# Half-precision pairs for the q, k and v projections of a cross-attention and expert-layer kernel

## What is computed

```python
xn = layernorm(x)                        # over the last axis, 512
q = einsum('oc,bct->bot', Wq, xn) + bq   # 256 x 256 weights, per batch row 256 x 512
k = einsum('oc,bcs->bos', Wk, ctx) + bk
v = einsum('oc,bcs->bos', Wv, ctx) + bv
# 16 heads of 16 channels, 512 x 512 scores per head
dot = mask * (q.T k) / 4 - (1 - mask) * 1e6
x = x + (softmax(dot) * mask) @ v
```

## Time and profile before

| | |
|---|---|
| time of 3 runs, median (range) | 726.11 us (725.21 to 729.36) |
| profiled execution: time | 723.49 us |
| profiled execution: span | 721.7 us |
| mean granted TensorE clock | 0.944 of full speed |
| busy share of the span: TensorE, VectorE, ScalarE, GpSimd | 87%, 72%, 62%, 44% |
| chain that ended last, by engine | TensorE 62%, VectorE 14%, ScalarE 8%, issue 8%, DMA 4%, GpSimd 3% |

### The profile page before, as it was taken

How to read it: one execution, slowest core, us unless ns; L and a number is a source line. 1 busy time by engine, 2 the same in 40 slices (tenths; PEclk the granted TensorE clock), 3 DMA queues, 4 the chain that set the end, 5 groups by cost and what they waited for, 6 DMA issues and landing times.

```text
span 721.7 us, 11922 instructions
## 1 busy us (share of the span) xinstructions
PE 626.2 (87%) x3864; PEld 257.7 (36%) x3864; DVE 516.8 (72%) x959; ACT 448.9 (62%) x608; POOL 320.9 (44%) x444
## 2 busy tenths in 40 slices
PE   4788999999999999999999987778899799999950
PEld 3623333323333323323323221124444466664420
DVE  2497788888888898888888898742748354444674
ACT  3654878877877877878887875663522377773000
POOL 5583335355355454444533504321824644431554
PEclk9857999999999999999999996799999999999995
DMA  8533254354354355354234320042995133332454
GB/s 302 174 111 99 70 161 128 105 150 129 103 151 133 111 140 147 98 139 134 96 88 132 113 72 30 31 109 84 197 224 106 51 111 114 121 111 74 153 166 140
DMA packets 65611, 88.61 MB, mean 123 GB/s; under 512 B 12576, under 2 KB 46112, under 8 KB 64528
## 3 DMA queue, kind: packets, MB, share of 16 engines
q1 hardware_dynamic: 60992, 69.64, 31.8%
q0 software_dynamic: 4560, 18.22, 10.9%
HBM read 63.75 MB, written 32.74 MB: 134 GB/s over the span
## 4 chain that ended last, share of the span: by engine, by line
PE 62%; DVE 14%; ACT 8%; issue 8%; DMA 4%; POOL 3%; SPq 0%; POOLq 0%; ACTq 0%; DVEq 0%
PE PS L859 16%; PE PS L831 10%; PE PS L640 8%; PE PS L766 8%; PE PS L1470 6%; ACT E L845 5%; DVE MX L772 5%; PE PS L719 4%; PE PS L1067 4%; PE PS L1531 3%; DVE ST L393 2%; POOL E L1583 2%; PE PS L1440 1%; DMA E<-scr_ys,SL 1%; ACT BIG L508 1%
## 5 line engine op out<-in xcount | busy, mean ns | idle before, releaser
L772 DVE TENSOR_REDUCE MX<-PS 128x1 f32<-128x512 f32 x512 | 327.0, 684 | 53.6 <-PE PS L766 53.0
L845 ACT ACTIVATE E<-PS 128x1024 f32<-128x1024 f32 x256 | 259.3, 1020 | 80.6 <-PE PS L831 79.7
L859 PE MATMUL PS<-E,BIG 128*32 128x512 f32 x1024 | 140.6, 622 | 3.3 <-ACT E L845 3.2
L766 PE MATMUL PS<-BIG 53*128 53x512 f16 x512 | 123.1, 400 | 17.5 <-DVE MX L772 17.2
L831 PE MATMUL PS<-BIG 55*128 55x512 f16 x512 | 103.0, 397 | 23.9 <-ACT E L845 20.7
L674 POOL TENSOR_TENSOR ML<-BIG,ML 128x512 f32<-128x512 f32 x30 | 38.2, 1275 | 142.5 <-ACT BIG L650 142.5
L831 PEld LDWEIGHTS PS<-BIG 55*128 55x128 f16 x512 | 24.6, 93 | 169.6 <-ACT E L845 99.7
L650 ACT ACTIVATE BIG<-PS,BIG 128x256 f32<-128x256 f32 x64 | 36.0, 564 | 34.4 <-PE PS L640 27.8
L1424 POOL DMA_INDIRECT CT<-scr_yr,IX x39 | 37.0, 949 | 43.3 <-PE PS L1440 36.3
L1492 DVE SCALAR_TENSOR_TENSOR E<-WP,PS 128x352 bf16<-128x352 f32 x39 | 20.3, 521 | 48.8 <-ACT WP L1482 46.1
L1470 PE MATMUL PS<-BIG,CT 128*128 x312 | 53.0, 313 | 2.3 <-ACT CT L1449 1.7
(11 more groups left out here) (207 smaller groups left out, 851.1 us busy)
## 6 DMA issues: line engine op xcount, KB each, us to landing
scr_parts<-WP SPq DMA_DIRECT2D x96, 128.0 KB
BIG<-scr_parts SPq DMA_DIRECT2D x64, 192.0 KB
BIG<-in_we POOLq DMA_DIRECT2D x8, 1088.0 KB, 13.9
scr_u<-ML SPq DMA_DIRECT2D x32, 256.0 KB, 2.2
scr_ys<-XN SPq DMA_DIRECT2D x19, 256.0 KB
X<-in_x SPq DMA_DIRECT2D x8, 512.0 KB, 6.0
CT<-in_ctx SPq DMA_DIRECT2D x8, 512.0 KB, 6.1
ML<-scr_u SPq DMA_DIRECT2D x16, 256.0 KB
```

What stands on the lines that cost most here:

```text
L766: e.matmul(PS[:, yi[name] % 3, :], QK[rows, qb(u), 0, j0 + jj, 128 * tt:128 * tt + 128], QK[rows, qb(u), 1, j0 + jj, :], start=True, stop= ...
L772: e.tensor_reduce(MX[:, g % 2, c:c + 1], PS[:, yi[name] % 3, :], AX.X, ALU.max)\
L845: e.activation(E[:, st, 2 * jj:2 * jj + 2, :], PS[:, slot(name):slot(name) + 2, :], ACT.Exp, scale=1 / 1024).then_inc(s["rc"], 1)
L859: ins = e.matmul(PS[32 * hh:32 * hh + 32, AVB, :], VT[:, b % 2, st, 4 * (g % 4) + hh, :], E[:, st, hh, :], start=(st == 0), stop=(st == 3))
```

## The change

In the profile's words, from unit 4 on (batch row 2 on), so in 12 of 16 units:

- `project_whole` takes the place of `project_qk`: q and k are computed for all 512 columns in one piece, as three float16 products per half of K (high by high, high by low, low by high), 6 matmuls of 128 x 512 instead of 4 float32 matmuls of 128 x 256. It takes one place in `ring` instead of two, due at 4.25 IT (q) and 7.25 IT (k), and is made before `attend`, so that at these due times it stands just ahead of an "a". ScalarE evacuates it in one piece of 512 columns.
- v takes 6 float16 matmuls of 256 columns per part instead of 2 float32 ones; its evacuation multiplies by a scale as well as adding the bias.
- `split_weights`, once: the sums of squares of the three weights (ScalarE, TensorE, VectorE, GpSimd), the high parts (ScalarE, three, due at 0.45 units) and the low parts (VectorE, three, due at 0.7 units).
- `split_source(b)`, for batch rows 2 to 7: five small GpSimd steps and three of 1024 columns (scale in place, high part, low part), due at 6.1 IT of the unit 2b - 4.
- `split_target(b)`: two GpSimd steps of 1024 columns, due at 0.3 IT of the unit 2b - 3. The normalised rows use one buffer from batch row 2 on, since the other one holds the pair.
- `balance` gets one small VectorE step and three small GpSimd steps for the new scales.
- The context of batch row 4 and later is loaded once the split of two rows earlier is done; two later users of the memory that holds the pairs wait for the last projections.

The diff, cut to its core:

```diff
+W0 = 4
...
+        ZW, WC, WI = few[:, 40:43], few[:, 43:46], few[:, 46:49]
+        CC, IC, VS, MS, RS = (few[:, i:i + 2] for i in (49, 51, 53, 55, 57))
+        WQs = big[:, 20672:23744].bitcast(HF).rearrange("p (r a b c) -> p r a b c", r=2, a=3, b=2)
+        CTs = [v.bitcast(HF).rearrange("p (r k t) -> p r k t", r=2, k=2)
+               for v in (big[:, 17792:19840], big[:, 15360:17408])]
+        XNs = XN[:, 1, :, :].rearrange("p k t -> p (k t)").bitcast(HF).rearrange("p (r k t) -> p r k t", r=2, k=2)
...
         for w in range(NU):
-            ring += [(w - 3 + 3.75 * IT, ("q", w, 0)), (w - 3 + 4.75 * IT, ("q", w, 1)),
-                     (w - 3 + 6.75 * IT, ("k", w, 0)), (w - 3 + 7.75 * IT, ("k", w, 1))]
+            if w < W0:
+                ring += [(w - 3 + 3.75 * IT, ("q", w, 0)), (w - 3 + 4.75 * IT, ("q", w, 1)),
+                         (w - 3 + 6.75 * IT, ("k", w, 0)), (w - 3 + 7.75 * IT, ("k", w, 1))]
+            else:
+                ring += [(w - 3 + 4.25 * IT, ("q", w, 1)), (w - 3 + 7.25 * IT, ("k", w, 1))]
             tv = -1 - .25 * IT if w == 1 else w - 2 + .75 * IT
             mring += [(tv, ("v", w, 0)), (tv + (.1 if w == 1 else 2) * IT, ("v", w, 1))]
         mring.append((-3 + 3.6 * IT, ("w",)))
         mring.append((-1.26, ("z",)))
+        mring.append((.12, ("y",)))
...
                 if n < 8:
-                    if n >= 2:
-                        e.wait_ge(s["rp"], zi["q", 2 * n - 3, 1] + 1)
-                    dst = XN[:, n % 2, :, :]
+                    if n == 2:
+                        e.wait_ge(s["rp"], zi["q", 1, 1] + 1)
+                    elif n > 2:
+                        e.wait_ge(s["xq"], n - 2)
+                    dst = XN[:, 1 if n == 1 else 0, :, :]
...
+                if b >= 4:
+                    e.wait_ge(s["cs"], b - 3)
+                if b >= 2:
+                    e.tensor_scalar(MS[:, b % 2:b % 2 + 1], PS[:, bank, 0:1], 1 / 131072, 1e-30, ALU.mult, ALU.max)
...
-                e.tensor_tensor(bq, bqkc[:, 0:2], r8, ALU.mult)
+                if b >= 2:
+                    pch.step(e, e.tensor_tensor(bq, bqkc[:, 0:2], r8, ALU.mult))
+                    e.tensor_tensor(r8, r8, WI[:, 0:1].broadcast_to([128, 2]), ALU.mult)
+                else:
+                    e.tensor_tensor(bq, bqkc[:, 0:2], r8, ALU.mult)
                 pch.step(e, e.tensor_scalar(sk, sk, 256.0, None, ALU.mult))
-                e.tensor_tensor(bk, bqkc[:, 2:4], sk, ALU.mult).then_inc(s["bal"], 1)
+                if b < 2:
+                    e.tensor_tensor(bk, bqkc[:, 2:4], sk, ALU.mult).then_inc(s["bal"], 1)
+                else:
+                    pch.step(e, e.tensor_tensor(bk, bqkc[:, 2:4], sk, ALU.mult))
+                    pch.step(e, e.tensor_tensor(sk, sk, WI[:, 1:2].broadcast_to([128, 2]), ALU.mult))
+                    e.tensor_tensor(sk, sk, IC[:, b % 2:b % 2 + 1].broadcast_to([128, 2]), ALU.mult)\
+                        .then_inc(s["bal"], 1)
...
+        def split_weights():
+            name = ("y",)
+            bank = yi[name] % 3
+
+            def squares(e):
+                e.wait_ge(s["w"], 32)
+                e.wait_ge(s["w1"], 16)
+                e.wait_ge(s["w2"], 16)
+                e.wait_ge(s["mp"], yi["w",] + 1)
+                spare = big[:, 20672:21696].bitcast(F32).rearrange("p (k c) -> p k c", k=2)
+                for i, out in enumerate((SQW[:, 0, :, :], SQW[:, 1, :, :], spare)):
+                    ins = e.activation(out, WQ[:, i, :, :], ACT.Square, accum_out=ZW[:, i:i + 1])
+                ins.then_inc(s["wz"], 1)
+            act.at(-.2, squares)
+
+            def mm(e):
+                take_bank(e, name)
+                e.wait_ge(s["wz"], 1)
+                e.matmul(PS[:, bank, 0:3], OO, ZW, start=True, stop=True).then_inc(s["mp"], 1)
+            pe.at(when_at[name], mm)
+
+            def fetch(e):
+                e.wait_ge(s["mp"], yi[name] + 1)
+                e.tensor_scalar(WC, PS[:, bank, 0:3], 1 / 65536, 1e-30, ALU.mult, ALU.max).then_inc(s["mc"], 1)
+            dve.at(when_at[name] + DA, fetch)
+
+            def factor(e):
+                e.wait_ge(s["mc"], yi[name] + 1)
+                pch.step(e, e.tensor_tensor(WC, WC, mhalf[:, 0:3], ALU.pow))
+                e.tensor_scalar(WC, WC, 64.0, None, ALU.mult).then_inc(s["wf"], 1)
+            pool.at(when_at[name] + .4 * IT, factor)
+
+            def upper(e):
+                e.wait_ge(s["wf"], 1)
+                e.wait_ge(s["sw"], 1)
+                for i in range(3):
+                    e.activation(WQs[:, 0, i, :, :], WQ[:, i, :, :], ACT.Identity, scale=WC[:, i:i + 1])\
+                        .then_inc(s["wh"], 1)
+            act.at(.45, upper)
+
+            def lower(e):
+                dch.step(e, e.reciprocal(WI, WC))
+                for i in range(3):
+                    e.wait_ge(s["wh"], i + 1)
+                    e.scalar_tensor_tensor(WQs[:, 1, i, :, :], WQ[:, i, :, :], WC[:, i:i + 1], WQs[:, 0, i, :, :],
+                                           ALU.mult, ALU.subtract).then_inc(s["wq"], 1)
+            dve.at(.7, lower)
+
+        def split_source(b):
+            name = ("f", b)
+            c, ic, v = CC[:, b % 2:b % 2 + 1], IC[:, b % 2:b % 2 + 1], VS[:, b % 2:b % 2 + 1]
+            ms, r = MS[:, b % 2:b % 2 + 1], RS[:, b % 2:b % 2 + 1]
+            src = CT[:, b % 2, :, :]
+            hi, lo = (CTs[b % 2][:, i, :, :] for i in range(2))
+
+            def factors(e):
+                if b == 2:
+                    e.wait_ge(s["wq"], 3)
+                if b >= 4:
+                    e.wait_ge(s["mc"], yi["v", 2 * b - 3, 1] + 1)
+                pch.step(e, e.tensor_tensor(r, ms, mhalf[:, 0:1], ALU.pow))
+                pch.step(e, e.tensor_scalar(c, r, 64.0, None, ALU.mult))
+                pch.step(e, e.tensor_tensor(ic, ms, r, ALU.mult))
+                pch.step(e, e.tensor_scalar(ic, ic, 1 / 64, None, ALU.mult))
+                e.tensor_tensor(v, ic, WI[:, 2:3], ALU.mult).then_inc(s["cs"], 1)
+            pool.at(when_at[name] + .312 * IT, factors)
+
+            def split(e):
+                e.wait_ge(s["sqa"], b + 1)
+                if b >= 4:
+                    e.wait_ge(s["rp"], zi["k", 2 * b - 3, 1] + 1)
+                elif b == 2:
+                    e.wait_ge(s["sw"], 3)
+                pch.step(e, e.tensor_scalar(src, src, c, None, ALU.mult))
+                pch.step(e, e.tensor_copy(hi, src))
+                e.tensor_tensor(lo, src, hi, ALU.subtract).then_inc(s["cq"], 1)
+            pool.at(when_at[name] + .34 * IT, split)
+
+        def split_target(b):
+            src = XN[:, 0, :, :]
+
+            def split(e):
+                e.wait_ge(s["xn"], b + 1)
+                e.wait_ge(s["rp"], zi["q", 2 * b - 1, 1] + 1)
+                pch.step(e, e.tensor_copy(XNs[:, 0, :, :], src))
+                e.tensor_tensor(XNs[:, 1, :, :], src, XNs[:, 0, :, :], ALU.subtract).then_inc(s["xq"], 1)
+            pool.at(2 * b - 4 + 8.3 * IT, split)
+
+        def project_whole(w, i):
+            b, o = w // 2, w % 2
+            name = ("qk"[i], w, 1)
+            bank = slot(name)
+            rows = XNs if i == 0 else CTs[b % 2]
+
+            def mm(e):
+                take_slot(e, name)
+                e.wait_ge(s["cq" if i else "xq"], b - 1)
+                if w == W0:
+                    e.wait_ge(s["wq"], i + 1)
+                for kt in range(2):
+                    for a, c in ((0, 0), (0, 1), (1, 0)):
+                        ins = e.matmul(PS[:, bank, :], WQs[:, a, i, kt, 128 * o:128 * o + 128], rows[:, c, kt, :],
+                                       start=(kt == a == c == 0), stop=(kt == a == 1))
+                ins.then_inc(s["rp"], 1)
+            pe.at(when_at[name], mm)
+
+            def evac(e):
+                e.wait_ge(s["rp"], zi[name] + 1)
+                e.wait_ge(s["bal"], b + 1)
+                e.wait_ge(s["fr%d" % i], w)
+                e.activation(FB[:, i, :], PS[:, bank, :], ACT.Identity,
+                             bias=COL[:, b % 2, 4 * i + 2 + o:4 * i + 3 + o],
+                             scale=COL[:, b % 2, 4 * i + o:4 * i + o + 1]).then_inc(s["rc"], 1)
+            act.at(when_at[name] + DA, evac)
+
...
+                    n = slice(128 * st, 128 * st + 128)
                     for kt in range(2):
-                        ins = e.matmul(PS[:, bank, 0:256], CT[:, b % 2, kt, 128 * st:128 * st + 128],
-                                       WQ[:, 2, kt, :], start=(kt == 0), stop=(kt == 1))
+                        if w < W0:
+                            ins = e.matmul(PS[:, bank, 0:256], CT[:, b % 2, kt, n],
+                                           WQ[:, 2, kt, :], start=(kt == 0), stop=(kt == 1))
+                            continue
+                        for a, c in ((0, 0), (0, 1), (1, 0)):
+                            ins = e.matmul(PS[:, bank, 0:256], CTs[b % 2][:, a, kt, n], WQs[:, c, 2, kt, :],
```

(29 more changed lines are left out.)

14 lines of the change are left out of this document (9 added, 5 removed), and 2 rows, old and new, of the table s.

## The result

The changed kernel takes 763.67 us (median of four runs, 761.39 to 765.84) against 727.36 of the kernel before in the same job: a ratio of 1.052, 95% interval 1.0486 to 1.0555. It is slower, as forecast, but by 36 us where the forecast said 15.5, and it lies above the range's 757.

What follows compares the result with a forecast made beforehand. Three engines near full, chained by two slots and three banks, bound the loop, not TensorE's columns alone. Projections 10.3 + 1.4 and weights 3.8 gave 15.5 us more, 741.6 against the median; range 729 to 757.

Steps and rivals of the forecast that it cites:

- What ends a step: Main loop: the second s waits for a bank, freed by VectorE's reduction, with "a" queued behind it.
- an empty step gives back 0.42: Steps that lose a projection half: each half costs TensorE 1.06 us but the loop only 0.42.
- a whole piece at this place fills nothing: Piece at 4.25 and 7.25 IT, behind the second s: "a" and all behind it move by the full 1.39 us.
- The 24 places: Whole q and k pieces: 19 at 0.54 us more, 5 with the context's squares at 0.28 more; 10.3 + 1.4 us.
- columns count in full: Rival, main loop: bound by TensorE's issue, 25 us less and 3.8 more for the weights, 705 us; chance 0.08.
- The weights' split, once: Unit 0: high parts and context squares on ScalarE 2.3 us, low parts on VectorE 1.5; together 3.8, between 0 and 6.5.
- The low parts: Weights' split on VectorE, unit 0: three at least 0.70 us each and a small step, delaying their step by 1.5 us.
- GpSimd ... its results are needed units later, so I cost it at 0: GpSimd's splits: about 10.5 us more per batch row, from 25.3 to 36 of a period of 54, cost 0.
- Loads on SyncE are not later than before: SyncE's queue: the change makes no load later, so no cost was counted.
- The first victim: GpSimd's added work: the ratio in `balance`, for which VectorE's reciprocal waits, was to lose its cover first.
- The clock falls: Rival: longer gaps in units with the squares drop TensorE's clock, 18 to 33 us more, 760 to 775; chance 0.1.
- Gain 0: v's step and the next, 3.31 us: shorter matmuls gain nothing, the second s being held by VectorE's reductions; at best 7 us.

Runs made afterwards that it cites:

- e6: Kernel before with the placing alone: one whole float32 piece at 4.25 and 7.25 from unit 4 on, no splits; 759.16 us, ratio 1.0438.
- e12: Changed kernel with context's split behind k's parts, weights' low parts spread, q and k as half-precision halves at their old places; 747.34 us, ratio 1.023.
- e17: e14 with the statistics of x moved on VectorE's queue from 5.6 to 4.35 eighths; 728.19 us, ratio 1.0047.
- e13: e9 with the weights' three low parts spread over VectorE's queue; 748.98 us, ratio 1.0367.
- e9: Changed kernel with GpSimd's context split moved behind the parts of k; 753.6 us, ratio 1.0357.
- e14: e13 with two small steps off VectorE: the maxima's high part on ScalarE, their low part left out; 751.07 us, ratio 1.0397.
- e2: Changed kernel with both row splits on GpSimd cut to 8 columns from batch row 4 on; 761.33 us, ratio 1.0505.
- e1: Changed kernel with the whole q and k pieces half a step earlier, at 3.75 and 6.75 IT; 765.1 us, ratio 1.0534.
- e3: Changed kernel with the weights' split moved ahead of the main loop; 764.2 us, ratio 1.0543.
- e4: Changed kernel with the edits of e1 and e3 together; 769.78 us, ratio 1.0604.

## Why the prediction was right in sign and short by more than half

**Right.** What ends a step (the second s, held by a reduction), that an empty step gives back 0.42, that a whole piece at this place fills nothing: 3.66 and 7.67 measured against 3.65 and 7.66, and e6 shows the same with another piece. The 24 places cost 10.8 us, forecast 11.7. Against the rival "columns count in full" stands e12 too. With the added troubles removed, the period agrees: e17 has 53.8, and with the 0.9 of the moved statistics added back 54.7, the forecast's number. One slip without effect: six matmuls at the 131 ns that it quotes from the Trainium skill are 0.79 us, 0.6 less than 1.39 and not 0.5; the piece took 1.39.

**Wrong: "The weights' split, once ... Together 3.8, between 0 and 6.5."** It cost 7.0, and 8.6 with the longer half clock at the loop's start (which may be chance: other kernels with the same code there lose 0.4); the other 4.6 of the stretch's 13.2 are GpSimd's. The low parts were put at "at least 0.70 each like the statistics"; they took 1.20 beside GpSimd (0.75 spread out), and the wait was charged as if the hole took a third of it, while TensorE stood for 2.87 and the clock fell behind: 6.3 us instead of 1.5. The high parts cost 0.7 instead of 2.3. With the low parts spread and the context's split moved (e13) the loop grows only by 1.6 up to the n at 107.2.

**Wrong: "GpSimd ... its results are needed units later, so I cost it at 0."** This is the step that failed, with 8.8 us in the place of 0, the largest of the terms that were mis-sized. GpSimd's amount was right (36.2 us busy in a period, forecast 36), what hangs on it was not. The work stands ahead of k's parts, whose store blocks SyncE's queue ahead of n's rows, 4.2 us; "Loads on SyncE are not later than before" looked at the loads and not at this store. And it makes VectorE's smallest steps up to ten times as long, 4.6 us at the n at 100 us. e9, which only moves the split in GpSimd's queue, removes both and gains 10 us. The first victim was not the ratio in `balance`.

**Wrong in weight: "The clock falls ... I give it 0.1."** It fell in four of five periods, at the statistics step, which the forecast used only as a price. (The measured time lies in this rival's 760 to 775, but by luck: the falls cost 3.4 us net, and not at the steps with the squares, where the rival had them.) That step grew from 2.44 to 2.95 because the x ahead of it comes sooner: the statistics start 0.69 us before it (178.96, x at 179.65) instead of 1.20, and all the rest of their length shows. The Trainium skill, TensorE: Matmul & The Clock Gate, "A second HAM failure mode", said that short idles can make the clock swing; the trace agrees, with waits of about 1 us (1.04 at 181.28) ahead of a fall. Moving the statistics ended the falls and gave 23 us in all (e14 to e17). Yet the same wait stands in e9 without a fall behind it:

```profile
292.75 0.39 PE L928 MATMUL PS<-BIG 53*128 53x512 f16 x1 [1.04 <-DVE MX L934]
```

So the gap alone does not decide (four of five such steps in e6 and two of five in e9 and e13 have no fall). What else does stays open.

**v: "Gain 0."** The second pair is exactly that, 1.30 + 2.00 = 3.30. The first lost 0.25 to 0.35, 3.7 us in all, to a small step held by GpSimd (e13 against e14), and by e6 this comes with the place of the whole piece.

The terms do not simply add. e14 removed a cause and gained nothing, because the next one grew; only the last of four cures brought the time near the kernel before. That the ratios of e13 and e9 or the medians of e2 and the changed kernel lie close says therefore little on each cause; the steps in the traces say it. The table of 37.9 us is read from one profiled execution of each kernel, and the share of the falls of the clock changes from one kernel to the next.

## What to carry to other kernels

Work added to an engine with much idle time is free only if two questions are answered from its queue: which instruction stands behind it and who waits for that one (a store that waits at the head of SyncE's queue counts), and which small instructions of a neighbour run beside it and are held until it ends. A long instruction that must go somewhere belongs behind the last short one that somebody waits for; here one moved line each was worth 10 and 23 us. And before making a matmul shorter, follow the chain through the slots: from x over its exponential to the next x it took 1.60 us, with or without the shorter half.

## What the hardware showed that I had not expected

- A VectorE step of 16 columns, 0.175 us alone, took 1.74 us (2.12 in e1) beside a GpSimd instruction and ended within 0.03 us of it; reductions from PS beside the same instructions kept their 0.62 (2.47 for four).
- Cutting a GpSimd instruction of 1024 columns into four costs 0.4 us (1.04 to 1.43, 2.13 to 2.55).
- Of the five statistics steps in the loop, the granted clock fell behind one in the kernel before and in e6, three in e9 and e13, four in the changed kernel and e14, none in e17, where the steps are 1.55 us long, although all but the first have heavy steps; a heavy step caught by it took up to 5.8 instead of 3.66.
- Ahead of the loop, the profiled executions differ by some us (its first step at 60 to 66 us, e3 and e4 left aside), so steps and periods were compared rather than positions.
